# First group's z from transposed tiles and float32 passes on TensorE, a thinner correlation bound, and the weight splits moved into the group's loop

## The reference, cut to what matters

```
xn = (x - mean) / sqrt(var + 1e-5)                  # along the 1024
corr = irfft(|rfft(xn)|^2); weights, delay = top_k(corr, 6)
s = sum_k softmax(weights)_k * xn shifted by delay_k
linear(x; w, A, B) = x @ tile(w, 4).T + 0.5 * (x @ A.T) @ B.T      # rank 2
g = silu(linear(silu(linear(xn; w1,a1,b1)) * linear(xn; w3,a3,b3); w2,a2,b2))
out = x + s * g
```

## Time and profile before

| | us |
|---|---|
| median of three runs | 945.19 |
| the profiled execution's own time | 945.45 |
| its span, first to last instruction | 943.7 |
| PE busy | 881.7 (93%) |
| DVE busy | 650.7 (69%) |
| ACT busy | 295.7 (31%) |
| POOL busy | 316.5 (34%) |

### The profile page before, as it was taken

How to read it: one execution, slowest core, us unless ns; L and a number is a source line. 1 busy time by engine, 2 the same in 40 slices (tenths; PEclk the granted TensorE clock), 3 DMA queues, 4 the chain that set the end, 5 groups by cost and what they waited for, 6 DMA issues and landing times.

```text
span 943.7 us, 11541 instructions
## 1 busy us (share of the span) xinstructions
PE 881.7 (93%) x4214; PEld 469.5 (50%) x4214; DVE 650.7 (69%) x1048; ACT 295.7 (31%) x432; POOL 316.5 (34%) x406
## 2 busy tenths in 40 slices
PE   5059988999999999999999999999999999999996
PEld 2023335744475345734476345844476345844465
DVE  5699997387945888377954979367954889343533
ACT  2545341243322332133322323133322333123221
POOL 4945551055502363044601373044700473000000
PEclk9988998999999999999999999999999999999999
DMA  9515121321224112321215022231114111220003
GB/s 282 146 34 209 34 56 23 112 90 34 63 58 163 29 34 51 113 90 34 57 26 188 17 58 51 91 113 34 56 23 167 37 40 29 81 100 1 1 0 136
DMA packets 53328, 69.80 MB, mean 74 GB/s; under 512 B 36969, under 2 KB 39145, under 8 KB 53105
## 3 DMA queue, kind: packets, MB, share of 16 engines
q1 hardware_dynamic: 53232, 68.75, 23.6%
HBM read 43.57 MB, written 16.78 MB: 64 GB/s over the span
## 4 chain that ended last, share of the span: by engine, by line
PE 84%; DVE 8%; issue 2%; DVEq 2%; POOL 2%; ACT 1%; DMA 1%; SPq 0%; ACTq 0%; POOLq 0%
PE g L917 23%; PE u L917 21%; PE g L1015 5%; PE u L1017 5%; PE u L1015 5%; PE g L1017 5%; PE u L1019 5%; PE g L1019 5%; PE zb L995 5%; PE g L936 4%; DVE junk L600 2%; PE mb L962 2%; PE mb L973 1%; DVE w_l L803 1%; DVEq L653 1%
## 5 line engine op out<-in xcount | busy, mean ns | idle before, releaser
L917 PE MATMUL g<-xt,w_h 128*128 128x512 f16 (+1 forms) x704 | 212.6, 384 | 15.9 <-DVE w_l L803 15.0
L917 PE MATMUL u<-xt,w_h 128*128 128x512 f16 (+1 forms) x704 | 210.6, 381 | 0.0
L455 ACT ACTIVATE sil<-g,winv 128x512 f32<-128x512 f32 (+1 forms) x176 | 119.4, 684 | 226.8 <-PE g L936 175.5
L637 DVE SCALAR_TENSOR_TENSOR h<-u,winv,sil 128x512 f32<-128x512 f32 (+1 forms) x176 | 130.5, 745 | 83.1 <-ACT sil L455 78.2
L600 DVE CUSTOM_DVE_ANT_0 junk<-xn,abc 128x1024 bf16<-128x1024 f32 x116 | 160.5, 1384 | 7.6 <-issue 2.2
L917 PE MATMUL g<-xt,w_l 128*128 128x512 f16 (+1 forms) x352 | 134.4, 382 | 0.0
L917 PE MATMUL u<-xt,w_l 128*128 128x512 f16 (+1 forms) x352 | 133.7, 380 | 0.0
L764 DVE SCALAR_TENSOR_TENSOR ob<-xr,c_mean,gg 128x1024 f32<-128x1024 f32 x32 | 41.1, 1285 | 117.9 <-ACT gg L455 117.9
L917 PEld LDWEIGHTS g<-xt,w_h 128*128 128x128 f16 (+1 forms) x704 | 61.5, 100 | 106.1 <-issue 53.3
L917 PEld LDWEIGHTS u<-xt,w_h 128*128 128x128 f16 (+1 forms) x704 | 70.8, 101 | 82.5 <-issue 1.8
L384 POOL TENSOR_TENSOR ve<-mv,three 128x1 f32<-128x1 f32 x32 | 7.5, 233 | 260.4 <-DVE mv L586 248.8
(11 more groups left out here) (117 smaller groups left out, 1234.8 us busy)
## 6 DMA issues: line engine op xcount, KB each, us to landing
xr<-in_x SPq DMA_DIRECT2D x34, 512.0 KB, 4.8
out_x<-ob SPq DMA_DIRECT2D x32, 512.0 KB, 2.9
xf<-in_x SPq DMA_DIRECT2D x30, 512.0 KB, 3.5
raw_w<-in_w2t SPq DMA_DIRECT2D x1, 3072.0 KB, 11.0
raw_w<-in_w1t SPq DMA_DIRECT2D x3, 768.0 KB, 9.7
raw_w<-in_w3t SPq DMA_DIRECT2D x3, 768.0 KB, 11.5
xt<-hl SPq DMA_TRANSPOSE x32, 2.5
ft<-ab SPq DMA_TRANSPOSE x32, 2.5
```

The source lines that it names most:

```text
L455: return nc.scalar.activation(out, in_, f, **kw)
L637: stt(out=h[0:n, p % NH, :], in0=ub[p % 3][0:n, :], scalar=winv[0:n, 2 * (p // 6) + 1:2 * (p // 6) + 2], in1=sil[0:n, p % 2, :], op0=ALU.m ...
L917: o = mm(bank[0:n, :], a, x, start=opens and t == 0, stop=closes and t == len(terms) - 1)
```

## The change

- **Correlation bound.** The table of 256 odd frequencies becomes one of 128, chosen by a constant bit mask; the bound that lag 0 must exceed goes from 160 to 112. `odd_power` has two steps instead of four (p = 5 and 9), `lags` has 4 passes a step instead of 8.
- **z of group 0.** The 16 `project` steps, `z_split` and `z_across` of group 0 are gone. TensorE turns a1 and a3 (8 small transposes) and the four normalised tiles (32 transposes of 128x128 into all eight banks); ACT and DVE copy four banks each to `xT`; TensorE makes z already transposed by eight float32 passes into one bank; ACT rounds it (`z_hi`), DVE writes `zst`. `abc`, needed from group 1 on, comes by one DMA that copies 16 KB to each of 128 partitions, ahead of the `xt` transposes in SP's queue.
- **Order.** POOL does the four `spread` first, and `sums` for tiles 0 and 1 only; DVE makes those of tiles 2 and 3 (`quarters`). Block 1 of w1, w3 and b moves from before the loop into it. Of w2, the six `w2_high` go together behind `gate(0, 15)`; three `w2_low` stay in the loop (p = 16, 18, 20), three go behind `folded_low(0, 5)`. `lora(0, 1)` has its usual place, so `up(0, 1)` waits for `zst`.

```diff
-GAP = 160.0
+NF = 128
+FREQS = 0xd572de56c7995422a316d99c91a36e97d54268dafbedb20d2a38062f384e642b
+GAP = 112.0
...
-        C_AT, I_AT = (3, 5, 7, 9), (11, 15)
+        C_AT, I_AT = (5, 9), (11, 15)
...
-        LOW_AT = {6 * b + k - 4: (b + 1, k) for b in (1, 2) for k in range(6)}
-        HIGH_AT = {1: 2, 6: 3}
-        W2_AT = 14
+        LOW_AT = {5 * b + k - 4: (b, k) for b in range(1, NB) for k in range(5)}
+        HIGH_AT = {0: 1, 4: 2, 9: 3}
+        W2_AT = {16: 0, 18: 1, 20: 2}
...
             sp.dma_start(a_raw[:], d["a13"]).then_inc(a_loaded, 16)
-            sp.dma_start(pick[:], d["pick"].rearrange("p (k c) -> p k c", k=4)).then_inc(a_loaded, 16)
+            sp.dma_start(ident[:], d["ident"]).then_inc(i_loaded, 16)
...
+            sp.dma_start(abc[:].rearrange("p r c -> p (r c)"),
+                         d["a13"].rearrange("r c -> (r c)").partition_broadcast(P)).then_inc(abc_loaded, 16)
-            for q in range(4):
+            for q in (2, 0, 3, 1):
                 xt_load(0, q)
...
+            for q in range(4):
+                spread(0, q)
+            sums(0, 0)
+            sums(0, 1)
+            nc.gpsimd.memset(zs[:], 0.0).then_inc(zeroed, 1)
...
+            for q in range(4):
+                normalise(0, q)
             w_bound(0)
+            for n, k in enumerate(XA):
+                act.wait_ge(x_ready, k + 1)
+                A(xT[:, k, :], x_banks[k][:], ACT.Copy).then_inc(xa_done, 1)
             w_high(0)
             b_high(0)
             for b in range(1, NB):
                 w_bound(b)
-            w_high(1)
-            z_copy(0)
-            b_high(1)
+            act.wait_ge(z0_ready, 1)
+            A(z_hi[:], mb[:], ACT.Copy).then_inc(z0_high, 1)
...
+                    if i == 0 and p == 15:
+                        for n in range(HN + 1):
+                            w2_high(n)
...
+            def quarters(q):
+                x, n = normal_buf(0, q), q - 2
...
+                tt(yh2[:], x[:, 0:HALF], x[:, HALF:L], ALU.add)
+                drain()
+                tt(xq2[:], yh2[:, 0:DQ], yh2[:, DQ:HALF], ALU.add)
+                drain()
+                copy(hl[:, q, 0:DQ], xq2[:])
+                drain()
+                tt(hl[:, q, DQ:HALF], xq2[:], hl[:, q, 0:DQ], ALU.subtract).then_inc(hl2_done, 1)
...
+            nc.vector.memset(aT[:], 0.0)
+            dve.wait_ge(a_ready, 1)
...
             for q in range(4):
                 stats(0, q)
+            quarters(2)
+            quarters(3)
+            x_copy(7)
             w_tops(0, 2)
+            x_copy(1)
             w_scale(0, 2)
+            x_copy(3)
+            x_copy(5)
             b_scale(0)
             for m in range(2):
                 for k in range(2):
                     w_low(0, m, k)
             b_split(0)
+            dve.wait_ge(z0_high, 1)
+            stt(out=zst[:], in0=z_hi[:].bitcast(F32), scalar=low[:, 0:1], in1=mb[:], op0=ALU.mult,
+                op1=ALU.add).then_inc(zst_done, 1)
+            nc.vector.memset(hf_h[96:P, HN, :].bitcast(F32), 0.0)
+            nc.vector.memset(hf_l[96:P, HN, :].bitcast(F32), 0.0)
             w_tops(2, 6)
             w_scale(2, 6)
...
                 folded_low(i, HN)
+                if i == 0:
+                    for n in range(len(W2_AT), HN + 1):
+                        w2_low(n)
...
-                for k in range(2):
-                    t = 2 * (c // 2) + k
+                for k in range(2):
+                    t = 2 * c + k
...
-                    for c in range(4):
-                        o = mm(mb[:, DQ * j:DQ * j + DQ], sq[:, c, t], inv[:, c % 2, :], start=c == 0, stop=c == 3)
+                    for c in range(2):
+                        o = mm(mb[:, DQ * j:DQ * j + DQ], sq[:, c, t], inv[:, 0, :], start=c == 0, stop=c == 1)
...
+            for k in range(8):
+                o = nc.tensor.transpose(mb[:, 4 * k:4 * k + 4], a_raw[:, k * P:(k + 1) * P], ident[0:4, 0:4])
+            o.then_inc(a_ready, 1)
+            for q in range(4):
+                pe.wait_ge(normed, q + 1)
+                if q == 0:
+                    pe.wait_ge(a_done, 1)
+                for k in range(8):
+                    o = nc.tensor.transpose(x_banks[k][:, q * P:(q + 1) * P],
+                                            normal_buf(0, q)[:, k * P:(k + 1) * P], ident[:])
...
 +                else:
+                    pe.wait_ge(xd_done, 1)
...
             w_tops(0, 2)
             w_tops_across(0, 2)
+            for n, k in enumerate((6, 7, 0, 1, 2, 3, 4, 5)):
+                pe.wait_ge((xa_done, xd_done)[n % 2], n // 2 + 1)
+                o = mm(mb[:], aT[:, k, :], xT[:, k, :], start=n == 0, stop=n == 7)
+            o.then_inc(z0_ready, 1)
...
-                    if i == 0 and p == 2:
-                        z_across(0)
-                        lora(0, 1)
```

More of the change, by code:

```diff
@@ L119, in build @@
         hl = sb("hl", [P, 4, HALF], F16)
+        junk_at = place[0]
         junk = sb("junk", [P, L], BF16)
@@ L192, in build @@
         a_raw = sb("a_raw", [4, L], F32, at=o_at)
-        pick = sb("pick", [4, 4, P], F32, at=o_at + 4096)
+        yh2 = sb("yh2", [P, HALF], F32, at=o_at + 4096)
+        xq2 = sb("xq2", [P, DQ], F32, at=junk_at)
+        xT = sb("xT", [P, 8, G], F32, at=hf_at)
+        aT = sb("aT", [P, 8, P], F32, at=hf_at + 16384)
+        z_hi = sb("z_hi", [P, G], F32R, at=hf_at + 20480)
         ones = sb("ones", [6, P], F32, at=o_at + 6144)
@@ L423, in _ @@
             nc.gpsimd.memset(ones[:], 1.0).then_inc(zeroed, 1)
-            nc.gpsimd.memset(zs[:], 0.0).then_inc(zeroed, 1)
[L425 to L436, removed]
+            pool.wait_ge(zeroed, 4)
+            for q in range(4):
+                spread(0, q)
+            sums(0, 0)
+            sums(0, 1)
+            nc.gpsimd.memset(zs[:], 0.0).then_inc(zeroed, 1)
             for q in range(4):
@@ L828, in w2_low, with x_copy @@
                 nc.vector.memset(w2_l[96:P, HN, :].bitcast(F32), 0.0).then_inc(w2l_done, 1)
+            def quarters(q):
+                x, n = normal_buf(0, q), q - 2
+                dve.wait_ge(normed, q + 1)
+                if n:
+                    dve.wait_ge(hl2_done, n)
+                else:
+                    dve.wait_ge(a_ready, 1)
[6 more added lines that the diff above has]
+                tt(hl[:, q, DQ:HALF], xq2[:], hl[:, q, 0:DQ], ALU.subtract).then_inc(hl2_done, 1)
+            def x_copy(k):
+                dve.wait_ge(x_ready, k + 1)
+                copy(xT[:, k, :], x_banks[k][:]).then_inc(xd_done, 1)
+            nc.vector.memset(aT[:], 0.0)
+            drain()
+            dve.wait_ge(a_ready, 1)
+            for s in range(4):
+                for u in range(3):
+                    c = 32 * s + 4 * u
+                    o = copy(aT[:, :, c:c + 4], mb[:, 0:32].rearrange("p (k r) -> p k r", k=8))
+            o.then_inc(a_done, 1)
             for q in range(4):
                 stats(0, q)
[L832 to L839, removed]
+            quarters(2)
+            quarters(3)
+            x_copy(7)
             w_tops(0, 2)
-            project(0, 1, 0)
+            x_copy(1)
             w_scale(0, 2)
-            for r in range(1, 4):
-                project(0, 1, r)
+            x_copy(3)
+            x_copy(5)
             b_scale(0)
@@ L849, in _ @@
             b_split(0)
-            for r in range(4):
-                project(0, 2, r)
+            dve.wait_ge(z0_high, 1)
[3 more added lines that the diff above has]
+            nc.vector.memset(hf_l[96:P, HN, :].bitcast(F32), 0.0)
             w_tops(2, 6)
-            project(0, 3, 0)
             w_scale(2, 6)
[L855 to L860, removed]
-                for k in range(2):
-                    w_low(1, m, k)
-            b_split(1)
+            dve.wait_ge(zeroed, 5)
             for i in range(NG):
@@ L927, in lora @@
             def lora(i, p):
-                first = i == 0 and p == 1
                 if p == 1:
@@ L936, in lora @@
                     o = mm((gb, ub)[s % 2][k % 3][0:n, :], bst[32 * s:32 * s + 32, p // 2, 0:n],
-                           zst[32 * s:32 * s + 32, :], start=s >= 2 and not first, stop=s < 2 or first)
-                    if s < 2 or first:
-                        o.then_inc((g_ready, u_ready)[s % 2], 1)
+                           zst[32 * s:32 * s + 32, :], start=s >= 2, stop=s < 2)
+                    if s < 2:
+                        o.then_inc((g_ready, u_ready)[s], 1)
             def up(i, p):
```

120 lines of the change are left out of this document (64 added, 56 removed).

## The result

The changed kernel takes 916.28 us (median of 4 runs, 915.53 to 916.54) against 945.3 for the kernel before beside it: the ratio is 0.9685, 95% interval 0.9667 to 0.9703. The forecast was 918 (908 to 932). The profiled execution took 916.3, its span is 914.5.

A forecast was written before the change was run, and what follows sets the result against it. TensorE was taken to bound groups 1 to 7 and VectorE's list group 0. From 945.45: −12.1 passes, −18.8 loop opening, +0.2 inside the loop, +0.5 xt, +3.2 behind the loop = 918.4, forecast 918, range 908 to 932.

The forecast's parts named there:

- Passes of the correlation: Groups 1 to 7: TensorE has no gap, so fewer passes save 1.73 us a group, 12.1 for seven.
- GpSimd's start: Group 0: POOL's first spread kept at 14.28 us; 1.6 earlier if its wait begins when the memsets end.
- The opening of the loop: Group 0's VectorE loop opens at 50.8 us instead of 69.6: gain 18.8, range 15 to 21.
- z on TensorE: Group 0: eight float32 z passes end by 36 to 40.7 us, hidden because z waits for ScalarE's bounds.
- abc's load: One 2 MB DMA ahead of xt: xt lands at 37 to 39 us, 0.5 late, up to 3.
- Inside the loop: Group 0's loop: block 1 and w2 moves sum to +0.2, so 83.6 us; TensorE, needing about 60, no bound.
- first rival: Group 0 gives most back through VectorE's dense list and ScalarE's w2 block: 931 us at worst, middle 926; chance 25%.
- Behind the loop: After group 0's loop: down's n = 3 waits 3.7 us for w2_low(3); +3.2 in all, between 0 and 5.
- The slow path: Correlation bound fails for any of 4096 rows (margin under 112): 5 ms for one group; chance 2%.
- Signs of being wrong: xt landing past 42, VectorE waiting over 3 us for ScalarE at p = 16, or loop over 88.
- steady groups: The sum's term for groups 1 to 7, fewer correlation passes on TensorE: 12.1 us less.
- the separate 0.5 for xt: The sum's term for the xt transposes landing late for up(0,0) behind abc's load: +0.5 us.

The follow-up runs named there:

- experiment 1: Kernel before with only the thinner correlation bound (128 frequencies, two odd_power steps, four passes a lags step, GAP 112): 935.52 us, ratio 0.9891.
- Experiment 2: Kernel before, two 32x512 memsets moved from GpSimd's start to VectorE: 942.17 us; changed kernel with three memsets put at GpSimd's start: 922.01 us.
- experiment 5: Changed kernel with the eight float32 z passes of group 0 made twice over: 916.18 us, ratio 0.9695.
- experiment 4: Changed kernel with the 2 MB load of abc issued behind the four xt transposes instead of ahead of them: 917.19 us, ratio 0.9696.
- Experiment 6: Changed kernel with each step of the weight splits in the loop one pair earlier (block 1 at p = 0 to 4): 909.1 us, ratio 0.9613.
- second kernel of experiment 2: Changed kernel with three memsets of zs (128x512, twice 32x512) at GpSimd's start in place of the later one: 922.01 us, ratio 0.9748.

## Why the prediction was right, point by point

The total was right within 2.1 us, and part of that is luck: errors of both signs, the largest 4.1 us, cancelled.

- **Passes of the correlation.** Forecast 1.73 a group and 12.1 in all. Measured 1.75 a group (107.11 to 105.36) and 13.8 over groups 1 to 7 and their end (ScalarE's copies of z: 166.03 to 810.14 before, 150.65 to 782.77 after, so 12.0; behind the last one 1.8). The mechanism was right; the term missed some 1.5 for two old groups with a wait of TensorE that the new order does not have: the 107.50 of 107.50 that it rested on was one group. In the old order the same passes bring 9.4 there (experiment 1).
- **GpSimd's start.** I kept 14.28 and put −1.6 as the most for the memsets. It was 7.89: the step was right in kind and mis-sized by four. The profile's 0.52 for each memset was the wrong row to size it by; of the 11.67 of idle behind them, some 6 were the cost of the three, with the waits between them. Experiment 2 shows it. With the start that I had kept (14.07) the kernel takes 922.0.
- **The opening of the loop.** 50.8 forecast, 46.66 measured, 53.0 where GpSimd starts at 14.07. The gain of 22.9 lies outside the 15 to 21 that I gave for it. I also added up the last step wrongly: 46.2 + 3.1 + 0.5 + 0.2 is 50.0, not 50.8. So the rest of my list was 2.2 short of what came, and 3.0 by its own terms. `quarters` took 3.7 a tile, not 2.6. The rule of the Trainium skill in "SBUF — State Buffer", Who interferes with whom, gave 3.0 and so had the right sign, and the trace agrees: the 128x256 sum above takes 1.48 beside a sum of GpSimd, where the sum of twice its width just before it takes 0.69. The copy, which my estimate by that rule left out, took 0.67 in place of 0.3. On the other side the block 0 remainders took 3.80 and not 5.74, as GpSimd stood 10.7 us for ft behind abc's load and left VectorE alone.
- **z on TensorE.** Forecast: hidden behind ScalarE's bounds at either clock. Right (z_hi at 37.91 behind the last bound, passes done at 32.2; experiment 5). The rule of the Trainium skill in "TensorE: Matmul & The Clock Gate", Part 4: PE-mode transpose, that transposes do not count for the clock, is not borne out here: among the 32 transposes, with nothing else on TensorE, the pitch goes from 0.21 to 0.11 at 13.2 us, and a pass from 0.42 to 0.27. (The view of the granted clock reads 1.00 here even while the pitch is 0.21, so the level is read from the pitch.) TensorE then stood from 16.2 to 21.2; the granted clock was 0.50 from 20.1 to 27.0, so the first z passes ran slow, and then 1.00, so the others did not. My step from that rule to "all z passes at 1.2 GHz" was wrong as well, as it speaks of transposes alone.
- **abc's load.** Forecast: xt at 37 to 39, up to 3 late. It landed at 35.95 and held `up(0,0)`; taken away, nothing is gained (experiment 4).
- **Inside the loop.** Forecast 83.6, measured 86.3. The step that failed is "TensorE, which needs about 60, is no bound there". In sum it is not; at one place it was: `up(0,6)` needs the whole of block 1, VectorE delivered it behind pair 4, TensorE stood 6.07 and came back at the lower clock, and VectorE then waited 3.43 for the gate behind it. Experiment 6 takes this away with the same work on every engine, and 7 us with it. The first rival named VectorE's dense list and the block of w2_high; the density was there, and the wait at p = 16 was 1.78, but with the splits earlier that went too, so what cost was the order.
- **Behind the loop.** Forecast +3.2. From the last product to the copy of z it is 17.7 against 13.1, so +4.6: the wait of 3.7 is there as forecast. The clock is the rest: TensorE works 5.3 us of this stretch at the lower level (137.7 to 143.0), where the kernel before had 3.4 (154.4 to 157.8).
- **The slow path** did not run, as forecast.
- **Signs of being wrong.** None of the three came: xt landed before 42, VectorE's wait at p = 16 was 1.78 and not over 3, the loop took 86.3 and not over 88. The 3.43 at `up(0,6)` stood at a place that they did not name.

The sum again with what was measured: opening −4.1, loop +2.7, steady groups −1.7, behind the loop +1.4, the separate 0.5 for xt gone: 2.2 less than the forecast. Measured is 2.1 less.

## What to carry to other kernels

A wait that the profile shows may be the cover of the next one: move a producer only after asking what is late behind it, and look at the clock of the engine that will idle. When a bound engine's list is full, the order in it decides as well as its length: give first what another engine needs as a whole (here the splits of each block one pair earlier, 7 us). And an idle stretch that no semaphore explains need not be a constant: here more than half of it was the cost of what stood ahead of it in the queue.

## What the runs showed that I had not expected

- Wide memsets at GpSimd's start, with the waits between them, delay its first arithmetic by about 2 us each (7.9 us with none, 10.1 with one, 14.1, 14.3 and once 15.65 with three), while the memset of zs later in the changed kernel (drawn from 20.91, 0.52 long) let the next instruction start at 21.39. Why the start is dearer was not found.
- Transposes alone brought TensorE to full pace: at 13.2 us in the changed kernel, and at 19.6 in the second kernel of experiment 2, where they start 6.2 later. The eight products of a1 and a3 with `pick` in the kernel before go at 1.71 each, the lower level, from the first at 2.93 to the last at 15.04.
- In experiment 4 the first pair's data came 3.5 us earlier; the second pair then ran at the lower clock and the loop opened 1.1 us later.
